# A two-layer graph kernel: transposes in 64-row halves and in pairs of tiles, and one value product moved

## What is computed

```
h = max(layernorm(x), 0)
x = x + attention(h, adj)            # 6 heads of 64; masked softmax(q k^T / 8) v, then Wf
h = max(layernorm(x), 0)
x = x + graph_attention(h, adj)      # 12 heads of 32

# graph_attention
hh = h @ W                            # features, by head
s, d = tanh(hh) . w_src, tanh(hh) . w_dst
a = softmax(leaky_relu(s_i + d_j, 0.2) where adj, else -999)
f = elu(a @ hh + b)
gate = sigmoid(h @ H_w.T + H_b)
out = gate * f + (1 - gate) * h
```

## Time and profile before

| | |
|---|---|
| time, median of 3 runs | 1798.54 us (1797.27 to 1798.77) |
| profiled execution | 1799.47 us, span 1797.7 us |
| granted TensorE clock, mean | 0.99 |
| busy: TensorE, VectorE | 1674.6 us (93%), 1335.1 us (74%) |
| busy: ScalarE, GpSimd | 1101.8 us (61%), 1033.7 us (58%) |
| chain that ended last | TensorE 72%, ScalarE 12%, VectorE 8%, issue 6%, GpSimd 1% |
| DMA | 46.46 MB, 26 GB/s mean |

### The profile page before, as it was taken

The page is one execution under the profiler, slowest core; times in us unless marked ns, Lnnn a source line. Parts: engine busy times, 40 slices in busy tenths (PEclk is TensorE's granted clock), DMA queues, the critical chain, the costliest instruction groups (busy, mean ns, idle before and its releaser), DMA issues.

```text
span 1797.7 us, 39493 instructions
## 1 busy us (share of the span) xinstructions
PE 1674.6 (93%) x12528; PEld 1021.2 (57%) x12528; DVE 1335.1 (74%) x3130; ACT 1101.8 (61%) x2231; POOL 1033.7 (58%) x1287
## 2 busy tenths in 40 slices
PE   5899999999999999999999999999999999999885
PEld 4464655647465574645657465574655646556461
DVE  4778687786878768677786877768777786876847
ACT  2666566665666656566665666666566665666653
POOL 4356565674656656565564646646565565655735
PEclk9899999999999999999999999999999999999998
DMA  4000101001010010100001010010100101000000
GB/s 155 19 19 12 49 6 35 18 14 44 6 51 7 13 39 6 53 6 21 32 10 48 6 35 23 9 44 6 53 6 13 39 9 50 6 18 19 10 10 18
DMA packets 38114, 46.46 MB, mean 26 GB/s; under 512 B 2624, under 2 KB 38080, under 8 KB 38080
## 3 DMA queue, kind: packets, MB, share of 16 engines
q1 hardware_dynamic: 38080, 46.03, 8.0%
HBM read 33.44 MB, written 12.58 MB: 26 GB/s over the span
## 4 chain that ended last, share of the span: by engine, by line
PE 72%; ACT 12%; DVE 8%; issue 6%; POOL 1%; DVEq 1%; DMA 0%; ACTq 0%; POOLq 0%
PE work L1099 16%; PE score L1099 16%; ACT arena L576 8%; PE acc L1258 8%; PE acc L1252 6%; PE acc L1190 5%; PE score L1156 4%; DVE arena L867 4%; PE work L1173 3%; PE work L1252 3%; PE score L1233 2%; PE acc L1211 2%; ACT arena L582 2%; PE score L1219 1%; PE work L1271 1%
## 5 line engine op out<-in xcount | busy, mean ns | idle before, releaser
L867 DVE SCALAR_TENSOR_TENSOR arena<-score,uqT,adjT 128x512 f32<-128x512 f32 x576 | 389.1, 744 | 35.7 <-PE score L1233 25.4
L416 POOL TENSOR_SCALAR arena<-arena,rinv 128x512 f32<-128x512 f32 x384 | 280.4, 746 | 185.8 <-DVE rinv L828 185.8
L576 ACT ACTIVATE arena<-sm,nmax 128x512 f32<-128x512 f32 x384 | 273.1, 713 | 128.8 <-DVE nmax L822 126.8
L450 POOL TENSOR_TENSOR arena<-arena,adjT 128x512 f32<-128x512 f32 x192 | 224.0, 1167 | 126.0 <-ACT arena L617 121.7
L822 DVE CUSTOM_DVE_ANT_0 sm<-score,mask 128x512 f32<-128x512 f32 x384 | 247.7, 685 | 60.4 <-PE score L1156 57.9
L1173 PEld LDWEIGHTS work<-ident_f,arena 64*128 64x128 f32 x3072 | 115.2, 140 | 185.9 <-issue 185.9
L1258 PE MATMUL acc<-arena,u_den 128*3 128x512 f32 x1536 | 200.8, 592 | 0.0
L1190 PE MATMUL acc<-arena,v_tok 128*64 128x512 f32 x768 | 198.7, 617 | 0.0
L423 POOL TENSOR_TENSOR rstd<-var,mhalf 128x1 f32<-128x1 f32 x128 | 68.7, 549 | 225.6 <-DVE var L786 225.6
L1173 PE MATMUL work<-ident_f,arena 64*128 64x64 f32 x3072 | 138.0, 229 | 60.5 <-ACT arena L582 40.9
L614 ACT ACTIVATE arena<-score,nqT 128x512 f32<-128x512 f32 x192 | 130.0, 677 | 103.3 <-PE score L1233 75.8
(11 more groups left out here) (168 smaller groups left out, 3952.2 us busy)
## 6 DMA issues: line engine op xcount, KB each, us to landing
x_in<-in_x SPq DMA_DIRECT2D x16, 768.0 KB, 4.6
xb<-in_x SPq DMA_DIRECT2D x16, 768.0 KB, 4.5
out_x<-xres SPq DMA_DIRECT2D x64, 192.0 KB, 1.9
adj_u<-in_adj SPq DMA_DIRECT2D x16, 256.0 KB, 2.8
arena<-in_wk SPq DMA_DIRECT2D x1, 576.0 KB, 6.1
arena<-in_wq SPq DMA_DIRECT2D x1, 576.0 KB, 7.2
arena<-in_wv SPq DMA_DIRECT2D x1, 576.0 KB, 8.5
arena<-in_wf SPq DMA_DIRECT2D x1, 576.0 KB, 9.5
```

What stands on the lines that cost most here:

```text
L416: nc.gpsimd.tensor_scalar(pr, pr, rinv[:, p, t, i:i + 1], 1.0, ALU.mult, ALU.mult).then_inc(probs_ready, 1)
L450: nc.gpsimd.tensor_tensor(edge_at(n, HG - 1), t_ring[:, n % 2], adjT[:, n % TT], ALU.mult).then_inc(last_edge_ready, 1)
L576: nc.scalar.activation(probs[p % 2 * 2 + i][:, t], sm[:, n % NSM], ACT.Exp, scale=-1.0, bias=nmax[:, p, t, i:i + 1], accum_out=rsum[:, p, ...
L867: nc.vector.scalar_tensor_tensor(out=edge_at(n, j), in0=score[j][:], scalar=uqT[:, c, q:q + 1], in1=adjT[:, c], op0=ALU.max, op1=ALU.mult) ...
```

## The change

- The second norm, the features and the sums are turned like the probabilities. Two tiles are taken together; of each, rows 0 to 63 go into the first bank of a pair and rows 64 to 127 into the second (`turn_halves`). Each bank then holds the same half of both tiles. For the features and the sums, "rows" are features and heads, so a bank holds half of the heads of two tiles.
- The readers follow: `turned_high2`, `turned_low2`, the copies to `h_tok`, `inverse_den` and `divide` take a half of two tiles at a time. The ReLU on the turned second norm, which was applied twice, falls away, as `hn` has it already.
- Heads are dealt to groups by `head_of`, so that each half of the turned sums and denominators holds the same heads.
- The banks of the values and of the turned sums change (`HOME`), and so does the order: the first value product of the next batch stands in front of the aggregation, the second in the middle of it, and the sums are turned in two goes, the second behind all value products. ScalarE's and VectorE's orders are changed to match, and the gate's tanh is spread out otherwise (`TANH_AT`).

The order on TensorE in the joint (of a product's nine matmuls the first and the last are shown): first the kernel before (L1156 scores, L1099 value products of batch b+1 from `wv`, L1271 and L1272 a turn of the sums), then the changed one (L1223 scores, L1147 value products, L1164 a turn of the sums, L1240 a turn of probabilities).

The diff, cut to its core:

```diff
+TANH_AT = {2: 1, 3: 2, 6: 3}
 SPREADS = (3, 0, 1, 2)
+def head_of(g, j):
+    return j // 2 * 2 * NG + 2 * g + j % 2
...
-    ("v", 0): 1, ("v", 1): 1, ("v", 2): 1, ("v", 3): 0,
+    ("v", 0): 0, ("v", 1): 1, ("v", 2): 0, ("v", 3): 1,
...
-    ("num", 1): 0, ("fin", 0): 0, ("fin", 1): 0, ("fin", 2): 1, ("fin", 3): 1,
+    ("num", 1): 0, ("fin", 0): 0, ("fin", 1): 1, ("fin", 2): 0, ("fin", 3): 1,
...
+        def halves(tensor, m):
+            pair, half = m // 2, m % 2
+            return tensor[:, :, pair * 2 * P:(pair + 1) * 2 * P].rearrange(
+                "p c (t h n) -> p t c h n", t=2, h=2)[:, :, :, half]
+        def turned(bank_, blocks):
+            return bank_[:, 0:2 * blocks * DH0].rearrange("p (t c n) -> p t c n", t=2, c=blocks)
...
+            def turned_high2(b, m):
+                filled(act, b, "norm2", m)
+                nc.scalar.activation(halves(hT_hi[1], m), turned(bank_of(b, "norm2", m), FC),
+                                     ACT.Copy).then_inc(hi_ready[1], 1)
...
-                    mark_drained(nc.scalar.activation(h_tok[:, t], bank_of(b, "tok", t)[:, 0:D], ACT.Copy),
-                                 b, "tok", t)
+                    mark_drained(nc.scalar.activation(
+                        h_tok[:, t // 2 * 2:t // 2 * 2 + 2].rearrange("p t (c h n) -> p t c h n", c=FC, h=2)[:, :, :, t % 2],
+                        turned(bank_of(b, "tok", t), FC), ACT.Copy), b, "tok", t)
...
-                    if n < 3:
-                        tanh_gate(b, n + 1)
+                    if more and n == 1:
+                        value(b + 1, 0)
+                    if n in TANH_AT:
+                        tanh_gate(b, TANH_AT[n])
                     if more and n == 4:
                         qk_hi_copy(b + 1, 2, "q")
                     if n % TT == 1 and n > 1:
                         sums_copy(b, n // TT - 1)
                     if more and n == 8:
-                        value(b + 1, 0)
+                        value(b + 1, 1)
                 if more:
                     exps(b + 1, 0, 0)
                 sums_copy(b, NG - 1)
                 if more:
-                    value(b + 1, 1)
                     exps(b + 1, 0, 1)
                     value(b + 1, 2)
                     exps(b + 1, 0, 2)
+                    value(b + 1, 3)
                     exps(b + 1, 0, 3)
-                    value(b + 1, 3)
                     exps(b + 1, 1, 0)
...
+            def turned_low2(b, m):
+                dve.wait_ge(hi_ready[1], b * TT + m + 1)
+                mark_drained(nc.vector.tensor_tensor(
+                    halves(hT_lo[1], m), turned(bank_of(b, "norm2", m), FC), halves(hT_hi[1], m).bitcast(F32),
+                    ALU.subtract), b, "norm2", m)
...
+            def inverse_den(b, m):
+                tiles, heads = slice(m // 2 * 2, m // 2 * 2 + 2), slice(m % 2 * 2 * NG, (m % 2 + 1) * 2 * NG)
+                filled(dve, b, "fin", m)
+                sums = turned(bank_of(b, "fin", m), NG + 1)[:, :, NG].rearrange("p t (j s) -> p t s j", j=2)
+                nc.vector.reciprocal(rden[:, tiles, heads].rearrange("p t (g j) -> p t g j", g=NG),
+                                     sums[:, :, 0:NG]).then_inc(rden_ready, 1)
+            def divide(b, m):
+                dve.wait_ge(rden_ready, b * TT + m + 1)
+                tiles, heads = slice(m // 2 * 2, m // 2 * 2 + 2), slice(m % 2 * 2 * NG, (m % 2 + 1) * 2 * NG)
                 mark_drained(nc.vector.tensor_tensor(
-                    fin_f[:, t].rearrange("p (a e) -> p a e", a=NH1),
-                    bank_of(b, "fin", t)[:, 0:D].rearrange("p (a e) -> p a e", a=NH1),
-                    rden[:, t].rearrange("p g j -> p (g j)").unsqueeze(2).to_broadcast([P, NH1, DH1]),
-                    ALU.mult), b, "fin", t)
+                    fin_f[:, tiles].rearrange("p t (a e) -> p t a e", e=DH1)[:, :, heads],
+                    bank_of(b, "fin", m).rearrange("p (t a e) -> p t a e", t=2, e=DH1)[:, :, 0:2 * NG],
+                    rden[:, tiles, heads].unsqueeze(3).to_broadcast([P, 2, 2 * NG, DH1]), ALU.mult), b, "fin", m)
...
-                for t in range(TT):
-                    if more and t < TT - 1:
-                        maxima(b + 1, 0, t + 1)
-                    if more:
-                        inverse(b + 1, 0, t)
-                    inverse_den(b, t)
-                    divide(b, t)
-                if more:
+                if more:
+                    maxima(b + 1, 0, 1)
+                    inverse(b + 1, 0, 0)
+                for m in range(2):
+                    inverse_den(b, m)
+                    divide(b, m)
+                if more:
+                    maxima(b + 1, 0, 2)
+                    inverse(b + 1, 0, 1)
+                    maxima(b + 1, 0, 3)
+                    inverse(b + 1, 0, 2)
+                for m in range(2, 4):
+                    inverse_den(b, m)
+                    divide(b, m)
+                if more:
+                    inverse(b + 1, 0, 3)
                     maxima(b + 1, 1, 0)
...
+            def turn_halves(banks, blocks, source):
+                for t in range(2):
+                    for c in range(blocks):
+                        for half in range(2):
+                            rows = slice(half * DH0, (half + 1) * DH0)
+                            at = (t * blocks + c) * DH0
+                            ins = nc.tensor.transpose(banks[half][0][:, at:at + DH0], source(t, c)[rows],
+                                                      ident_f[rows, rows])
+                            if (t, c) == (1, blocks - 1):
+                                mark_full(ins, *banks[half][1])
...
+            def turn_norm2(b, pair):
+                for half in range(2):
+                    bank_free(pe, b, "norm2", 2 * pair + half)
+                pe.wait_ge(hn_ready, b * TT + 2 * pair + 2)
+                settle(pe)
+                turn_halves([(bank_of(b, "norm2", 2 * pair + half), (b, "norm2", 2 * pair + half)) for half in range(2)],
+                            FC, lambda t, c: hn[:, 2 * pair + t, c * P:(c + 1) * P])
...
+            def turn_sums(b, pair):
+                if pair == 0:
                     pe.wait_ge(num_drained, START + (b + 1) * 2)
                     drained(pe, b, "num", 1)
                     pe.wait_ge(den_drained, b + 1)
-                bank_free(pe, b, "fin", t)
-                ps = bank_of(b, "fin", t)
-                for g in range(NG):
-                    nc.tensor.transpose(ps[:, g * P:(g + 1) * P], numT[:, g, t * P:(t + 1) * P], ident_f[:])
-                mark_full(nc.tensor.transpose(ps[:, D:N], denT[:, t * P:(t + 1) * P], ident_f[:]), b, "fin", t)
+                for half in range(2):
+                    bank_free(pe, b, "fin", 2 * pair + half)
+                settle(pe)
+                turn_halves([(bank_of(b, "fin", 2 * pair + half), (b, "fin", 2 * pair + half)) for half in range(2)], NG + 1,
+                            lambda t, c: (numT[:, c] if c < NG else denT)[:, (2 * pair + t) * P:(2 * pair + t + 1) * P])
...
-                turn_norm(b, 1, 0)
-                turn_norm(b, 1, 1)
+                turn_norm2(b, 0)
                 if more:
                     query_key(b + 1, 0, "q")
-                turn_norm(b, 1, 2)
-                turn_norm(b, 1, 3)
+                turn_norm2(b, 1)
...
                 gate_product(b, 3)
+                if more:
+                    values(b + 1, 0)
 
                 for n in range(STEPS):
...
                     if more and n == 1:
                         query_key(b + 1, 2, "q")
                     if more and n == 5:
-                        values(b + 1, 0)
+                        values(b + 1, 1)
                     if n in (1, 5):
 
                         for j in SPREADS:
                             spread(b, n // TT + 1, j)
                 if more:
                     scores(b + 1, 0, 1)
-                    values(b + 1, 1)
                 turn_sums(b, 0)
                 if more:
                     scores(b + 1, 0, 2)
                     values(b + 1, 2)
+                    scores(b + 1, 0, 3)
+                    values(b + 1, 3)
                 turn_sums(b, 1)
                 if more:
-                    scores(b + 1, 0, 3)
-                turn_sums(b, 2)
-                if more:
-                    values(b + 1, 3)
-                turn_sums(b, 3)
-                if more:
                     scores(b + 1, 1, 0)
```

More of the change, by code:

```diff
@@ L1214, in logits, with turn_feat @@
                     ins.then_inc((logits_b_full, logits_full)[c - 1], 1)
-            def turn_feat(b, t):
-                bank_free(pe, b, "tok", t)
-                for c in range(FC):
-                    ins = nc.tensor.transpose(bank_of(b, "tok", t)[:, c * P:(c + 1) * P],
-                                              feat[:, c, t * P:(t + 1) * P], ident_f[:])
-                mark_full(ins, b, "tok", t)
+            def turn_feat(b, pair):
```

(9 more changed lines are left out.)

113 lines of the change are left out of this document (54 added, 59 removed).

## The result

The changed kernel takes 1841.74 us (median; 1834.12 to 1847.69) against 1797.9 (1797.1 to 1798.77): ratio 1.0241, 95% interval 1.0196 to 1.0287. It is slower, as forecast, but by 44 us instead of 11, and outside the range. The profiled execution took 1837.38 us, its span 1835.6. In the old kernel the same point is at 968.04, so "+26.20" means 26.20 us behind it in either.

What follows compares the result with a forecast made beforehand. TensorE, busy for 93% of the span, was taken to bound the kernel, with its few waits. 0.07 + 0.66 = 0.73 us for 15 batches (+10.9), less 1 for the last, made 1799.47 + 10 = 1809.4; forecast 1809, range 1791 to 1838.

Steps and rivals of the forecast that it cites:

- Feature transposes: TensorE's turn of the features, in 64-row halves, takes 0.92 us per batch, saving 0.37, rounded to 0.36.
- Second norm: Turning the second norm in halves gains nothing, hidden by the wait for hT_lo: 0, bounds -0.05 and +0.2 per batch.
- Value product in front: Before the first aggregation step, 1.58 us of value product goes, with the 0.36 gain, into waits.
- The head's 0.07: The start of the aggregation comes out 0.07 us late per batch, bounds 0.36 early and 0.3 late.
- Joint: Between aggregation and next attention, the turn of the probabilities comes 0.66 us late, with TensorE standing for 2.5 us.
- Its own range is 1803 to 1815: The forecast's own range in us, with an error of 0.3 to 0.4 per batch.
- The sum: 0.07 + 0.66 = 0.73 us for 15 batches, +10.9, and -1 for the last batch: 10 us more.
- Falling clock: Rival: TensorE's clock falls in the new stall, about 2.6 us each; in 8 of 15 batches 1830 us; chance 0.29.
- the row of the late fall: Old profile, 1725.80 to 1729.20: TensorE busy 1.16 of 3.40 us, then granted clock 0.50 for 6.40 us.
- my stall: TensorE's predicted 2.5 us wait ahead of the turned probabilities; 0.9 us of work in a stretch of 3.40.
- absorbed: Rival: ScalarE works ahead, its 0.95 us wait shrinks by the turn's lateness, only the head counts: 1798.6 us; chance 0.16.
- faster: Rival: the joint is no longer than before and the head fits into its waits: 6.4 less, 1792 us; chance 0.16.

Runs made afterwards that it cites:

- a_norm2_full: The changed kernel with the second norm turned at full size as before, everything else as changed: 1827.15 us, ratio 1.0168.
- feat_only: The kernel before with only the features turned in 64-row halves in pairs of tiles: 1793.59 us, ratio 0.9974.
- b_stall: The kernel before with GpSimd held up by 40 semaphore increments ahead of its last normalise for each batch's first turned probabilities: 1858.11 us, ratio 1.0332.
- b_stall_short: The kernel before with GpSimd held up at the first turned probabilities by 15 semaphore increments: 1815.84 us, ratio 1.0099.
- feat_unrolled: The kernel before with the features turned in halves and TensorE's loop written out: 1791.01 us, ratio 0.9958.
- c_candidate: The changed kernel with the second norm at full size, the last probabilities ahead of the last two divides, and TensorE's loop written out: 1792.59 us, ratio 0.9978.
- a_unrolled: The changed kernel with TensorE's loop over the 14 middle batches written out: 1815.28 us, ratio 1.0102.
- b_padded: The kernel before with 90 more semaphore increments per batch in TensorE's loop body, spread between matmuls: 1849.95 us, ratio 1.0297.
- b_pad_ahead: The kernel before with 90 semaphore increments directly ahead of TensorE's loop, body untouched: 1827.21 us, ratio 1.0154.
- b_shifted_90: The kernel before with 90 semaphore increments at the very start of TensorE's program, same loop body: 1813.22 us, ratio 1.0071.

## Why the prediction was wrong

- **Feature transposes: right.** 0.89 us (forecast 0.92); alone they bring the aggregation's last step forward by 0.39 (0.36).
- **Second norm: wrong, small.** Forecast 0, bounds up to +0.2; a_norm2_full puts it at +0.26. The features' products start at +7.10 instead of +6.90. The cover that I named, VectorE's last hT_lo, was 0.2 us deep and stayed where it was; the wait of 0.51 for the pair's second tile made TensorE's own work the later of the two.
- **Value product in front: right.** The head's 0.07 was 0.43 for it less 0.36 for the features; a_norm2_full (+52.23) against feat_only (+51.79) makes it 0.44. With the norm's 0.26 the head is 0.31 late.
- **Joint: right.** 14.45 us from the last aggregation step to the turned probabilities against 13.75, +0.70 (forecast 0.66), with a wait of 2.59 (2.5), in the order that I walked. The wait is TensorE's for GpSimd, behind VectorE's four operations on the sums.
- **"Its own range is 1803 to 1815": wrong.** The sum held only what instructions and waits do in order. Without what falls and issue waits cost the 14 periods the span would be 1835.6 - 14.3 - 12.4 = 1808.9, where the sum has 1797.7 + 10 = 1807.7; the norm's 3.9 too much is about made up by a start and an end that are 4.5 shorter, which I had at 1.
- **Falling clock: right in kind, given too small a chance, and mis-sized.** Falls came in 14 of 15 batches; I took 8 as the middle of this case and gave it 0.29. I gave the row of the late fall more length (6.40 us) than most have, and too little to ScalarE's waits: 2.6 each, where the periods show 0.1 to 1.2. That my figure for a fall in all 15 batches, 1848, lies near the measured 1841.7 is luck: it has 39 us of falls, where the falls at the turns took about 11, and the loop, which it doesn't have, made up for them. b_stall shows that the wait makes the fall. I had argued that the 0.9 us of work in my stall weighs more, not being transposes, and makes the fall less likely. It came all the same: 0.81 us of busy time in 3.40, scores in good part, was followed by half clock. What the Trainium skill says there of transposes, that they don't count as busy in the same way (TensorE: Matmul & The Clock Gate, PE-mode transpose), no run here tests, as b_stall and the changed kernel have both kinds of work ahead of their falls.
- **The step that failed** is that the loop stays as cheap to jump back to as before. I counted the 40 matmuls more per batch as work and never as code: with their weight loads and increments they make the loop body 86 instructions longer. The sum has no term for that, without a reason given. The runs show 8 of 13 jumps back waiting, 12.4 us in the profiled execution, and 26 us less with the loop written out. It is also the step that took the time out of the range: written out, the change costs 17 us.
- The two rivals "absorbed" and "faster" are refuted for this change; a joint that is late is passed on (b_stall_short), and the joint was no shorter. The features alone do make the kernel faster, by 4.4 us, without any change to the joint.

What stays open: what the exact position of the body in its packets is (s was inferred, not read), why the same jump waits in one turn and not in the next, why the waits are short (0.3 to 0.9) in the two bodies that reach furthest, and why no further jump of the changed kernel waited after 988.16 us in the profiled run, where no packet was fetched from 1084 to 1649 us either. What activity makes the clock fall was not measured.

## What to carry to other kernels

Count the instructions that an edit adds to a hardware loop, and look at the instruction queue's packets and at issue waits behind the jump back before trusting a sum of durations; if the body grew past what stays, shorten it or write the loop out. A wait of 1 to 3.6 us on TensorE cost its length here and then, where the clock fell, another 0.1 to 1.2 us; part of the work lost to the clock vanished in waits that the following stage had anyway. Test the parts of a mixed change apart: here one part (the features) was worth -4.4 us and the others together hid it.

## What the runs showed of the hardware

- Written out, TensorE's programs of 26,693, 27,237 and 27,621 instructions (feat_unrolled, c_candidate, a_unrolled) came in 104, 106 and 107 packets of 16 KB, so a packet holds 256 instructions of 64 bytes. Fetching straight on made no wait that could be told from the looped kernel's; a jump back to code no longer held meant a wait of 0.3 to 2.9 us and about nine packets, and 0.25 us more behind it.
- Bodies of 1744 and 1770 instructions stayed for all 13 jumps back; 1804 and 1830 were fetched anew at some of them.
- The same code in another place can be dearer: 90 increments at the start, where TensorE idles anyway, made 10 of 13 jumps wait (+14 us), and 256 none.
- The clock fell behind a wait in a dense stretch in 0 of 15 batches at 0.71 us, 5 at 1.62, 14 at 2.59 and 15 at 3.57; such a fall cost 0.1 to 1.2 us. A fall behind a wait at the jump back cost 1.4 to 1.6 (b_padded, b_pad_ahead, b_shifted_90).
- A semaphore increment took 0.12 us on TensorE in a burst, nothing between matmuls, and 0.07 on GpSimd (2.87 us for 40).
- Written out, the loop also takes 0.2 us less per batch (108.17 against 108.35 for the features' version).
